# A four-layer gated cross-attention kernel: the order of single engine parts, down products by tokens, norms in pairs, and one product on GpSimd

## The chip, the cores and the metric

The kernel runs on one core of one Trainium2 chip. Its time is in microseconds (us) on the device, from the start of the program to its end, the median of some runs. The profile is that of one execution, and its span goes from the first to the last instruction of the program.

The engines are TensorE (PE in the rows, PEld for its weight loads), VectorE (DVE), ScalarE (ACT), GpSimd (POOL) and SyncE (SP, which only issues transfers).

## The reference, cut to what matters

Two batch elements ("halves", b = 0 and 1) of 512 tokens by 128 features go through four layers, each a cross-attention and a feed-forward part, both added to `x` with a gain of tanh:

```python
x = x + jnp.tanh(g_xattn[0]) * _L0_xattn_ref(_layernorm(x), ctx, ctx, mask, ...)   # stage 0: 16 heads of 8, 77 keys
x = x + jnp.tanh(g_ffn[0]) * _L0_ffn_ref(_layernorm(x), w1, b1, w2, b2)            # stage 1: relu, width 512
x = x + jnp.tanh(g_xattn[1]) * _L1_xattn_ref(_layernorm(x), ctx, ctx, ...)         # stage 2
x = x + jnp.tanh(g_ffn[1]) * _L1_ffn_ref(_layernorm(x), ...)     # stage 3: 16 experts of 64, top 2, a shared part of 352
x = x + jnp.tanh(g_xattn[2]) * _L2_xattn_ref(_layernorm(x), ctx, ctx, ...)         # stage 4
x = x + jnp.tanh(g_ffn[2]) * _L2_ffn_ref(_layernorm(x), ...)     # stage 5: 32 experts of 32, top 1, relu twice
x = x + jnp.tanh(g_xattn[3]) * _L3_xattn_ref(_layernorm(x), ctx, ...)  # stage 6: slot attention, 3 GRU steps
x = x + jnp.tanh(g_ffn[3]) * _L3_ffn_ref(_layernorm(x), rhs)     # stage 7: product of int8 values
```

Nothing in it crosses from one half to the other, so the halves may run in any order against each other. Within a half each stage needs the one before.

## The kernel before, in words

All of `x` stays in SBUF as four tiles of 128 tokens for each half. A stage begins with `norm` (VectorE: four `bn_stats`, four `bn_aggr`; GpSimd: variance plus epsilon to the power of minus a half, L698 and L699), `norm_end` (VectorE: four tiles of `xn`, L1315) and `turn` (TensorE: four transposes, L838; ScalarE: the copy `xn_t`, features on the partitions). An attention then goes `query`, `maxima` (four steps; VectorE takes the maxima of 16 blocks, L1443), `max_rows`, `scores` (three steps, each four eviction instructions of ScalarE with the exponential), `values` (three steps of sums and values together), `sum_rows`, `spread` (reciprocal sums spread with four full fp32 products, `rinv_d` against the identity), `project`. A feed-forward part has first products (`hidden0`; `shared` and `experts`; `hidden2`) and down products (`down0`, `down_shared` and `down1`, `down2`). The down products leave features on the partitions: a chunk is one fp32 product of 512 columns with the weights as the stationary side. ScalarE copies the sum to SBUF, TensorE transposes it back (`back`, L956), and VectorE adds it to `x` (L1346, L1542). A GRU step (`it` = 0 to 2) is `square`, `slots_turn` (L1052), `slot_products` (VectorE L1575), `slot_scores` (L1079, VectorE L1581), `hidden`, `slot_inverse`, four steps `gru` (VectorE L1609 and L1610), `gru_r` (VectorE L1616, L1617), `gru_z` (ScalarE, then VectorE L1622: `z` times the old slots) and `gru_end` (VectorE L1626, L1627). The last stage (L1324 to L1330, L1639) rounds to int8 values on VectorE.

Every engine runs a list of steps in fixed order (`ORDERS`). `schedule()` makes these lists when the program is built, from costs written beside each step. It walks three streams (half 0, half 1, preparation) and takes a step of a stream only in that stream's own order, with a few steps marked `on` or `side` that may overlap. `LATER` moves each step by a number of tenths. PSUM has eight banks, dealt by the same planner. Where it expects TensorE to be idle for long ahead of a step that takes a bank, it puts in fillers: bf16 products of 512 columns of constants (`psum<-halves` in the rows), whose result nobody reads. There are 178 of them: 33 ahead of the first `slots_turn`, 72 from there to the last `gru`, 73 in the last stage. All matrix products go through the helper on L754, and most ScalarE copies through L1124. Transfers are issued by SyncE in one list.

## Time and profile before

| | |
|---|---|
| median of 3 runs | 361.77 us (360.57 to 361.87) |
| the profiled execution | 361.95 us |
| its span | 360.2 us |
| TensorE busy | 328.1 us, 91% |
| VectorE busy | 225.3 us, 63% |
| ScalarE busy | 136.9 us, 38% |
| GpSimd busy | 47.8 us, 13% |

Busy time of TensorE counts the fillers too, and each product up to its modelled end, so two products in a pipeline overlap.

### The profile page before, as it was taken

How to read it: one execution, taken by the hardware profiler on the slowest of the kernel's cores; microseconds unless marked ns; L12 is line 12 of the kernel's file. 1: busy time of each engine (PE TensorE's matmuls, PEld its weight loads, DVE VectorE, ACT ScalarE, POOL GpSimd, SP SyncE). 2: the span in 40 equal slices, each digit the busy share in tenths (PEclk: the TensorE clock that was granted, in tenths of full speed). 3: DMA queues.
4: the chain of work that ended last, by engine and by line, in shares of the span. 5: the costliest groups of instructions: out<-in, count | busy, mean ns of one | idle time of the engine just before them, and what ended most of it. 6: DMA issues, size and time to landing. Idle time of an engine off the chain costs nothing.

```text
span 360.2 us, 5043 instructions
## 1 busy us (share of the span) xinstructions
PE 328.1 (91%) x1843; PEld 175.3 (49%) x1843; DVE 225.3 (63%) x635; ACT 136.9 (38%) x287; POOL 47.8 (13%) x73
## 2 busy tenths in 40 slices
PE   0789989998888899999999997899999999999994
PEld 0455453463424543554444434455445677677442
DVE  2596574366628551677766728345353797798995
ACT  1226326331451565225321361711232366646200
POOL 6113112031010100010200020101021311101110
PEclk9999999998989999999999999999999999999998
DMA  7940000000000000000000300000000000000001
GB/s 195 354 198 0 2 0 2 1 0 3 0 2 0 2 0 0 2 0 1 1 2 0 118 11 0 2 0 2 0 0 0 2 1 2 0 2 0 0 14 47
DMA packets 6669, 8.68 MB, mean 24 GB/s; under 512 B 2907, under 2 KB 5493, under 8 KB 6389
## 3 DMA queue, kind: packets, MB, share of 16 engines
q1 hardware_dynamic: 6645, 8.37, 7.0%
q8 instruction: 15, 0.25, 0.3%
q14 instruction: 9, 0.07, 0.1%
HBM read 7.84 MB, written 0.52 MB: 23 GB/s over the span
## 4 chain that ended last, share of the span: by engine, by line
PE 76%; DVE 15%; ACT 6%; issue 1%; DMA 1%; SPq 0%; DVEq 0%; ACTq 0%
PE psum L754 68%; DVE mx L1443 6%; ACT wide L1124 4%; PE psum L838 3%; DVE wide L1610 1%; PE psum L956 1%; PE psum L874 1%; DMA w_attn<-in_attn 1%; PE psum L1052 1%; PE psum L1079 1%; ACT xn_t L1124 1%; PE psum L791 0%; DVE rinv_d L1452 0%; DVE wide L1575 0%; DVE rinv L1449 0%
## 5 line engine op out<-in xcount | busy, mean ns | idle before, releaser
L754 PE MATMUL psum<-xn_t,w_ffn 128*128 128x512 f32 (+1 forms) x136 | 66.6, 608 | 0.8 <-ACT xn_t L1124 0.8
L754 PE MATMUL psum<-wide,w_ffn 128*128 128x512 f32 (+1 forms) x92 | 47.4, 603 | 0.5 <-DVE wide L1535 0.3
L754 PE MATMUL psum<-halves 128*128 128x512 bf16 x178 | 43.9, 379 | 0.2 <-DVE q_lo L1435 0.2
L1443 DVE TENSOR_REDUCE mx<-psum 128x4 f32<-128x308 f32 x96 | 38.7, 471 | 7.3 <-PE psum L754 7.1
L1124 ACT ACTIVATE wide<-psum 128x512 f32<-128x512 f32 x72 | 36.6, 624 | 11.0 <-PE psum L754 10.8
L1124 ACT ACTIVATE q<-psum 128x512 f32<-128x512 f32 (+1 forms) x40 | 23.5, 594 | 44.1 <-PE psum L754 43.8
L754 PEld LDWEIGHTS psum<-xn_t,w_ffn 128*128 128x128 f32 (+1 forms) x136 | 24.9, 190 | 28.8 <-issue 25.9
L698 POOL TENSOR_SCALAR nw<-mv 128x4 f32<-128x4 f32 x16 | 3.6, 227 | 218.7 <-DVE mv L1309 218.7
L754 PEld LDWEIGHTS psum<-halves 128*128 128x128 bf16 x178 | 17.3, 99 | 17.2 <-issue 1.7
L1315 DVE TENSOR_SCALAR xn<-x,mv,nw 128x128 f32<-128x128 f32 x64 | 17.8, 347 | 10.9 <-POOL nw L699 10.7
L754 PE MATMUL psum<-w_attn,q 128*128 128x128 f32 x192 | 23.7, 276 | 0.2 <-DVE q L1459 0.2
L754 PEld LDWEIGHTS psum<-wide,w_ffn 128*128 128x128 f32 (+1 forms) x92 | 16.3, 192 | 15.0 <-issue 8.5
L754 PEld LDWEIGHTS psum<-w_attn,q 128*128 128x128 f32 x192 | 22.5, 192 | 2.0 <-issue 1.1
L1124 ACT ACTIVATE xn_t<-psum 128x512 f32<-128x512 f32 x18 | 11.1, 615 | 30.5 <-PE psum L838 16.5
L1124 ACT ACTIVATE wide<-psum,cols 128x512 f32<-128x512 f32 x12 | 8.2, 687 | 31.2 <-PE psum L754 31.2
L754 PE MATMUL psum<-wide,heads_of 128*32 128x512 f32 x144 | 20.0, 626 | 0.0
L754 PE MATMUL psum<-wide,v_cols 128*32 128x512 f32 x144 | 19.6, 614 | 0.0
L1528 DVE TENSOR_TENSOR wide<-q,psum 128x512 f32<-128x512 f32 x16 | 11.0, 685 | 11.4 <-PE psum L754 9.8
L754 PE MATMUL psum<-wide 78*128 78x386 f32 x48 | 17.8, 496 | 0.2 <-DVE wide L1598 0.2
L699 POOL TENSOR_TENSOR nw<-nw,minus_half 128x4 f32<-128x4 f32 x16 | 16.6, 1036 | 1.3
L1306 DVE BATCH_NORM_STATS2 stats<-x 128x6 f32<-128x128 f32 x64 | 13.9, 280 | 3.9 <-DMA x<-in_x 3.5
L1435 DVE SCALAR_TENSOR_TENSOR q_lo<-psum,cols,q_hi 128x512 fp32r<-128x512 f32 x6 | 4.5, 751 | 18.5 <-ACT q_hi L1180 18.5
(208 smaller groups left out, 492.5 us busy)
## 6 DMA issues: line engine op xcount, KB each, us to landing
w_ffn<-in_ffn SPq DMA_DIRECT2D x1, 2088.5 KB, 12.6
w_ffn<-in_ffn SPq DMA_DIRECT2D x1, 1104.0 KB, 5.0
w_attn<-in_attn SPq DMA_DIRECT2D x1, 640.0 KB, 8.1
w_attn<-in_attn SPq DMA_DIRECT2D x2, 288.0 KB, 5.8
x<-in_x SPq DMA_DIRECT2D x2, 256.0 KB, 3.1
w_ffn<-in_ffn SPq DMA_DIRECT2D x1, 512.0 KB, 6.7
out<-x SPq DMA_DIRECT2D x2, 256.0 KB, 2.3
rows<-in_rows SPq DMA_DIRECT2D x1, 468.0 KB, 6.0
```

The lines of the kernel that those rows point to most:

```text
L699: G.tensor_tensor(nw[:, b, 2, :], nw[:, b, 0, :], minus_half[:, :], ALU.pow)\
L754: return nc.tensor.matmul(out_, lhs, rhs, start=start, stop=stop, **kw)
L838: last = nc.tensor.transpose(bk[:, t * P:(t + 1) * P], (y if stage == 7 else xn)[:, b, t, :], ident)
L874: last = nc.tensor.transpose(bk[:, t * P:(t + 1) * P], mx[:, b, t, :], ident)
L956: last = nc.tensor.transpose(bk[:, t * P:(t + 1) * P], tile[:, b, t * P:(t + 1) * P], ident)
L1052: last = nc.tensor.transpose(bk[:, t * P:(t + 1) * P], slots[:, b, t, :], ident)
L1124: A.activation(dst, banks.bank(*name)[0:rows_, 0:cols_], fn, **kw).then_inc(drained["act"], 1)
L1306: last = V.bn_stats(stats[:, b, t, :], x[:, b, t, :])
L1315: last = V.tensor_scalar(xn[:, b, t, :], x[:, b, t, :], mv[:, b, t, 0:1], nw[:, b, 2, t:t + 1], ALU.subtract, ALU.mult)
L1435: V.scalar_tensor_tensor(q_lo[:, b, :], banks.bank("q", layer, b), col(f"bq{layer}"), q_hi[:, b, :].bitcast(F32), ALU.add, ALU.subtract).t ...
L1443: last = V.tensor_reduce(mx[:, b, t, lane_heads(g)], banks.bank("max", layer, b, t, g)[:, 0:GK].rearrange("p (h k) -> p h k", k=CTX), AX.X ...
L1528: V.tensor_tensor(wide[:, b, c, :], act_s[slot][:, b, :], banks.bank("e_u", b, c), ALU.mult)\
```

## The change

1. **The planner** takes single engine parts: one step of one engine, with a list of the parts that it must follow. There are no streams any more; whichever part ranks first is next, whatever half it is of. The rank has the time at which a part can begin, `LATER` (new numbers, now for each part) and a fifth of the length of the chain that follows it. A change of TensorE's tiling (whole array, rows, columns) is charged 0.095 in the plan. `sums` and `values` are steps of their own, so are `gate` and `up` (the two first products of a piece), and the three products of `hidden`.
2. **Down products by tokens**: the hidden values are the stationary side and the weights the moving one, four products of 128 columns in place of one of 512, on top of a product of zeros that clears the bank. The sum has tokens on the partitions, and VectorE adds it to `x` from PSUM: the copy on ScalarE and the transposes of `back` go (in stage 5 the ReLU on ScalarE stays). `spread` becomes four transposes.
3. **Norms in pairs** of tiles: GpSimd and `norm_end` begin after two tiles, so GpSimd has twice the instructions.
4. **`z` times slots** (six instructions) goes from VectorE to GpSimd. In the last stage ScalarE scales and rounds, VectorE clamps.
5. **Fillers** may stand ahead of any TensorE part, in the bank that is free first. There are 101: 28 ahead of the first `slots_turn`, 9 from there to the last `gru`, 64 in the last stage. Eight more products stand at the start.
6. **Transfers** have another order, the identity and the query weights first, `x` of half 1 later; the weights of stage 5 are loaded after both `down0`, over the masks and the weights of layer 0.

The core of the diff:

```diff
+LEAD = {("pe", "turn"): 0.3}
+LEFT = 0.2
+SWITCH = 0.095
...
 def schedule():
...
+    waiting = list(steps.values())
+    while waiting:
         best = None
...
+        for st in waiting:
+            if all(steps[key].end is not None for key in st.after):
+                at = max([steps[key].end for key in st.after], default=0.0) - LEAD.get(st.key[:2], 0.0)
+                at = max(at, free[st.engine], LOADED.get(st.key, 0.0))
+                if st.engine == "pe" and tiling(st.phase, st.args)[0] != tiled:
+                    at = max(at, free["pe"] + SWITCH)
...
+                if at < float("inf"):
+                    rank = at + st.later - LEFT * st.left
...
+        if st.engine == "pe":
+            units = units_of(st.phase, st.half, st.args)
+            if at > FILL_FROM:
+                (bank, earlier), since = banks.first_free(drained)
+                idle = at - max(free["pe"], since) - FILLER
+                if idle >= FILLER:
+                    fillers[st.key] = bank, earlier, int(idle / FILLER)
...
             load_x(0)
+            sp.dma_start(cols[:, :], a["cols"]).then_inc(loaded["cols"], 16)
+            sp.dma_start(consts[:, 0:P], a["consts"][:, 0:P]).then_inc(loaded["ident"], 16)
+            sp.dma_start(packs["attn0"][:, 0:wq_n], a["attn0"][:, 0:wq_n]).then_inc(loaded["wq0"], 16)
...
             for b in range(B):
-                sp.wait_ge(*banks.full("y", 3, b))
+                sp.wait_ge(*banks.full("out", 1, b))
...
+            def norm(b, stage, h):
+                tiles = slice(2 * h, 2 * h + 2)
+                pool.wait_ge(var_ready[b], 2 * stage + h + 1)
+                link(G.tensor_scalar(nw[:, b, 0, tiles], mv[:, b, tiles, 1], LN_EPS, None, ALU.add))
+                G.tensor_tensor(nw[:, b, 2, tiles], nw[:, b, 0, tiles], minus_half[:, tiles], ALU.pow)\
...
+            def gru_z(b, it):
+                pool.wait_ge(z_ready[b], it + 1)
+                G.tensor_tensor(kept[:, b, :, :], tz[:, b, :, :], slots[:, b, :, :], ALU.mult).then_inc(kept_ready[b], 1)
...
-                    last = mm(bk[:, t * P:(t + 1) * P], rinv_d[:, b, t, :], ident)
+                    last = nc.tensor.transpose(bk[:, t * P:(t + 1) * P], rinv_d[:, b, t, :], ident)
...
                 pe.wait_ge(*banks.emptied(source, b, i))
-                done = mm(bk, weights[0:n, i * D:(i + 1) * D], wide[0:n, b, at_, :], start=i == 0, stop=last)
+                if i == 0:
+                    mm(bk, zeros16[:, :], halves[:, 0:S], stop=False)
+                by_tokens(bk, wide[0:n, b, at_, :], weights[0:n, i * D:(i + 1) * D], last)
+
+            def by_tokens(bk, source, weights, last):
+
+                for t in range(T):
+                    done = mm(bk[:, t * P:(t + 1) * P], source[:, t * P:(t + 1) * P], weights, start=False,
+                              stop=last and t == T - 1)
...
-            def back(b, stage):
-
-                pairs = [("s_out", ("s_y", b), s_y_t)] if stage == 3 else []
-                for name, source, tile in pairs + [("out", ("y", stage, b), y_t)]:
-                    bk = start_unit(name, *([stage] if name == "out" else []), b)
-                    pe.wait_ge(*banks.emptied(*source))
-                    for t in range(T):
-                        last = nc.tensor.transpose(bk[:, t * P:(t + 1) * P], tile[:, b, t * P:(t + 1) * P], ident)
-                    last.then_inc(filled, 1)
...
+            pe.wait_ge(idle_made, 1)
+            for _ in range(WARM_UP):
+                mm(psum[:, BANKS - 1, :], idle_t[:, 0:P], idle_t[:, :])
             for phase, b, args in ORDERS["pe"]:
+                if ("pe", phase, b, *args) in IDLE_FILLERS:
+                    keep_warm(*IDLE_FILLERS["pe", phase, b, *args])
...
+            def scaled(b):
+                act.wait_ge(centre_ready[b], 1)
+                for t in range(T):
+                    last = A.activation(xn[:, b, t, :], x[:, b, t, :], ACT.Identity, bias=nw[:, b, 0, t:t + 1],
+                                        scale=nw[:, b, 2, t:t + 1])
```

How the change moves instructions shows at two places. A row names the line, the operation, what is written, what is read (the moving side first) and the shape.

TensorE, stage 3 of half 1, before: the first products of a piece (`w_ffn1`, `experts`), the product that spreads the router's weights (`sel1`, `weigh`) and a down product (`wide,w_ffn1`, `down1`) take turns, and a step of `maxima` (`keys_hi,q_hi`) of half 0 stand between.

```order
L754 MATMUL psum<-wide,w_ffn1 128x512
L754 MATMUL psum<-keys_hi,q_hi 128x308 x4
L754 MATMUL psum<-xn_t,w_ffn1 128x512 x2
L754 MATMUL psum<-comb_t,sel1 128x512
L754 MATMUL psum<-wide,w_ffn1 128x512
L754 MATMUL psum<-xn_t,w_ffn1 128x512 x2
L754 MATMUL psum<-comb_t,sel1 128x512
```

TensorE, stage 3, now: the end of the first products of half 0, after those of half 1, then `weigh` and `down1` of both halves in turns.

```order
L854 MATMUL psum<-xn_t,w_ffn1 128x512 x8
L1104 MATMUL psum<-consts,comb 32x128 x4
L854 MATMUL psum<-xn_t,w_ffn1 128x512 x2
L854 MATMUL psum<-halves,zeros16 128x512
L854 MATMUL psum<-w_ffn1,wide 128x128 x4
...
L854 MATMUL psum<-comb_t,sel1 128x512 x7
L854 MATMUL psum<-halves,zeros16 128x512
L854 MATMUL psum<-w_ffn1,wide 128x128 x4
L854 MATMUL psum<-comb_t,sel1 128x512
L854 MATMUL psum<-w_ffn1,wide 128x128 x4
```

Both halves now do stage 3 side by side, ahead of any attention of stage 4, with no filler among these rows.

VectorE, GRU, before: `slot_scores` of one half (L1581), `gru_r` of the other (L1616, L1617), `z` times slots (L1622), `slot_inverse` (L1597, L1598), `hidden` (L1588), `gru_end` (L1626, L1627) and `gru`.

```order
L1581 TENSOR_REDUCE nmax<-psum 77x1
L1616 TENSOR_TENSOR wide<-wide 128x512
L1617 TENSOR_TENSOR wide<-wide 128x512
L1622 TENSOR_TENSOR q<-wide,xn 128x512
L1588 SCALAR_TENSOR_TENSOR wide<-psum,hidden_bias 128x4x128
L1597 RECIPROCAL nmax<-nmax 77x1
L1598 TENSOR_SCALAR wide<-vw,nmax 78x386
L1626 SCALAR_TENSOR_TENSOR xn_t<-wide,xn_t 128x512
L1627 TENSOR_TENSOR xn<-q,xn_t 128x512
```

VectorE, GRU, now:

```order
L1679 TENSOR_TENSOR wide<-psum,nw 128x308
L1685 TENSOR_REDUCE nmax<-psum 77x1
L1720 TENSOR_TENSOR wide<-wide 128x512
L1721 TENSOR_TENSOR wide<-wide 128x512
L1701 RECIPROCAL nmax<-nmax 77x1
L1702 TENSOR_SCALAR wide<-vw,nmax 78x386
L1692 SCALAR_TENSOR_TENSOR wide<-psum,hidden_bias 128x4x128
L1728 SCALAR_TENSOR_TENSOR xn_t<-wide,xn_t 128x512
L1729 TENSOR_TENSOR xn<-q,xn_t 128x512
```

The product of `z` and the slots is gone from VectorE; the rest keeps nearly the same turns between the halves.

## Rows read from the trace of the kernel before

**Rows 1.** The page: busy time, share and instructions of each engine.
```profile
PE 328.1 (91%) x1843; PEld 175.3 (49%) x1843; DVE 225.3 (63%) x635; ACT 136.9 (38%) x287; POOL 47.8 (13%) x73
```

**Rows 2.** The page: chain that ended last, share of the span.
```profile
PE 76%; DVE 15%; ACT 6%; issue 1%; DMA 1%; SPq 0%; DVEq 0%; ACTq 0%
```

**Rows 3.** Windows: length; PE, PEld, DVE, ACT, POOL busy; granted clock.
```profile
77.40:122.80 45.40, 39.41 (x251) 18.03 (x248) 27.42 (x83) 16.51 (x32) 7.59 (x9) 0.92 0.00 1
122.80:204.80 82.00, 81.58 (x316) 38.96 (x316) 49.86 (x136) 31.16 (x52) 3.81 (x5) 1.00 0.01 3
204.80:271.60 66.80, 61.69 (x374) 30.89 (x374) 33.06 (x99) 25.93 (x52) 8.02 (x12) 1.00 0.04 15
271.60:338.40 66.80, 65.78 (x380) 44.72 (x379) 52.50 (x127) 32.73 (x92) 9.00 (x15) 1.00 0.00 1
84.50:88.00 3.50, 3.50 (x9) 1.23 (x8) 2.29 (x5) 0.00 (x0) 0.00 (x0) 0.51 0.02 5
```

**Rows 4.** Timeline of the start: start, length, engine, line, what, count.
```profile
8.28 0.79 DVE L679 TENSOR_TENSOR keys_hi<-k_hi,lane_mask 128x616 fp32r<-128x616 f32 x1
8.44 1.71 POOL L679 TENSOR_TENSOR keys_lo<-k_lo,lane_mask 128x616 fp32r<-128x616 f32 x1 [2.18 <-DVE k_lo L1357]
8.99 1.33 DVE L1361 TENSOR_SCALAR minus_max<-lane_mask 128x308 fp32r<-128x308 f32 x1
10.25 1.10 DVE L1315 TENSOR_SCALAR xn<-x,mv,nw 128x128 f32<-128x128 f32 x4
17.04 6.26 DVE L1443 TENSOR_REDUCE mx<-psum 128x4 f32<-128x308 f32 x16 [0.90 <-PE psum L754]
```

**Rows 5.** Groups by line: names, shapes, count; busy us, mean ns.
```profile
L754 PE MATMUL psum<-halves 128*128 128x512 bf16 x178 | 43.9, 379 | 0.2 <-DVE q_lo L1435 0.2
L754 PE MATMUL psum<-consts,rinv_d 128*128 128x128 f32 x48 | 6.7, 283 | 2.8 <-DVE mx L1443 2.5 <-DVE rinv_d L1452 0.3
L754 PEld LDWEIGHTS psum<-w_attn,q 128*128 128x128 f32 x192 | 22.5, 192 | 2.0 <-issue 1.1 <-DVE q L1459 0.8
L699 POOL TENSOR_TENSOR nw<-nw,minus_half 128x4 f32<-128x4 f32 x16 | 16.6, 1036 | 1.3
L1622 DVE TENSOR_TENSOR q<-wide,xn 128x512 f32<-128x512 f32 x6 | 4.1, 683 | 0.0
```

**Rows 6.** Timeline: one fp32 product and its follower; `slots_turn`; one set of `hidden`.
```profile
264.51 1.02 PE L754 MATMUL psum<-xn_t,w_ffn 128*128 128x512 f32 x2
265.37 0.38 PE L754 MATMUL psum<-nothot_t,halves 128*128 128x512 bf16 x1
271.63 0.60 PE L1052 MATMUL psum<-consts,xn 128*128 128x128 f32 x4
288.00 2.84 PE L754 MATMUL psum<-w_attn,q 128*128 128x128 f32 x24
```

**Rows 7.** Timeline, attentions: end of the first; an eviction set; a query; later scores.
```profile
62.84 1.04 PE L754 MATMUL psum<-wide,v_cols 128*32 128x512 f32 x8
102.42 2.06 ACT L1124 ACTIVATE wide<-psum 128x512 f32<-128x512 f32 x4
105.26 1.13 PE L754 MATMUL psum<-xn_t,w_attn 128*128 128x512 f32 x2
106.42 0.69 ACT L1180 ACTIVATE q_hi<-psum,cols 128x512 fp32r<-128x512 f32 x1 [1.94 <-PE psum L754]
204.75 0.50 PE L754 MATMUL psum<-q_lo,keys_hi 32*128 32x512 f32 x4
```

**Rows 8.** Timeline: first and last `gru` end of five half-steps; VectorE beside GpSimd.
```profile
287.67 0.62 DVE L1610 SCALAR_TENSOR_TENSOR wide<-psum,route_s,wide 128x384 f32<-128x384 f32 x1
337.84 0.62 DVE L1610 SCALAR_TENSOR_TENSOR wide<-psum,route_s,wide 128x384 f32<-128x384 f32 x1
56.28 1.28 POOL L707 TENSOR_TENSOR x<-x,gbias 128x512 f32<-128x512 f32 x1 [1.23 <-DVE xn L1315]
56.31 1.27 DVE L1407 TENSOR_SCALAR p_small<-p_small 77x2 int32<-77x2 int32 x1
```

More of the change, by code:

```diff
@@ new lines, in all_steps, with chain, step, of @@
+def all_steps():
+    steps = {}
+    def chain(b):
+        def step(phase, *args, after=(), then=None, **takes):
+            previous = list(after)
+            for engine, us in takes.items():
+                key = engine, phase, b, *args
+                steps[key] = Step(key, us, previous + (then or {}).get(engine, []))
+                previous = [key]
+        return step
+    prepare_steps(chain(PREPARATION))
+    for b in range(B):
+        half_steps(b, chain(b))
+    return steps
+def of(b):
+    return lambda engine, phase, *args: (engine, phase, b, *args)
@@ L162, in attention @@
+        step("max_rows", layer, after=[at("dve", "maxima", layer, T - 1)], pe=0.45, act=0.5)
         for j in range(NJ):
-            step("scores", layer, j, on=True, pe=0.95 if layer else 1.95, act=1.95, after=[(PREPARATION, "masks")])
+            ready = [at("act", "max_rows", layer), at("dve", "query", layer), prepared("pool", "keys_in", layer)]
+            if not layer:
+                ready.append(prepared("act", "masks"))
+            step("scores", layer, j, after=ready + in_order("pe", "scores", layer, j), pe=0.95 if layer else 1.95, act=1.95)
@@ L172, in stream_steps @@
+        step("sum_rows", layer, after=[at("act", "sums", layer, NJ - 1)], pe=0.44, dve=0.92)
+        step("spread", layer, after=[at("dve", "sum_rows", layer)], then={"dve": [at("act", "values", layer, NJ - 1)]},
+             pe=0.44, dve=0.6)
+        step("project", stage, layer, after=[at("dve", "spread", layer)], then={"dve": [at("pool", "bias", stage)]},
+             pe=0.88, dve=0.65)
+        norm(stage + 1, [at("dve", "project", stage, layer)])
     norm(0)
     attention(0, 0)
-    step("bias", 1, side=True, pool=1.2, after=[(PREPARATION, "out_bias")])
@@ L233, in stream_steps @@
[L233 to L247 removed]
+    bias(1)
+    turn(1)
+    for m in range(C0):
+        step("hidden0", m, after=[at("act", "turn", 1)] + in_order("pe", "hidden0", m), pe=0.86,
+             **{"act" if m % 2 else "dve": 0.62})
+        down("down0", m, C0, [at("act" if m % 2 else "dve", "hidden0", m)])
@@ new lines, in half_steps @@
+    norm(4, [at("dve", "back_shared"), at("dve", "back", 3)])
+    attention(4, 2)
+    turn(5)
+    step("router", after=[at("act", "turn", 5)], pe=0.92, dve=1.74)
+    step("choice_turn", after=[at("dve", "router")], pe=0.43, act=0.5, dve=0.33)
+    for c in range(C2):
+        step("hidden2", c, after=[at("act", "turn", 5)] + in_order("pe", "hidden2", c), pe=0.86)
+        step("choose", c, after=[at("pe", "hidden2", c), at("dve", "choice_turn")] + in_order("pe", "choose", c), pe=0.22,
+             **{"act" if c % 2 else "dve": 0.62})
+        down("down2", c, C2 + 1, [at("act" if c % 2 else "dve", "choose", c)])
@@ new lines, in half_steps @@
+    step("slots_back", after=[at("dve", "gru_end", ITERS - 1)], dve=0.65)
+    norm(7, [at("dve", "slots_back")])
+    turn(7)
+    step("quantised", after=[at("dve", "turn", 7), prepared("dve", "slots_in", 4)], pe=0.25, dve=1.83)
+def schedule():
+    steps = all_steps()
+    for b, tenths in LATER.items():
+        for st, later in zip([st for st in steps.values() if st.half == b], tenths):
+            st.later = later / 10
+    followers = {key: [] for key in steps}
+    for st in steps.values():
+        for key in st.after:
+            followers[key].append(st)
+    for st in reversed(list(steps.values())):
+        st.left = st.us + LANDS[st.engine] + max([other.left for other in followers[st.key]], default=0.0)
```

633 lines of the change are left out of this document (305 added, 328 removed), and 49 rows, old and new, of the table LATER.

## The prediction

> **What bounds the kernel now.** I read four views, from wide to narrow. The page says who is busy: TensorE 91% of the span, VectorE 63%, nobody else half [rows 1]. The chain that ended last says who sets the end: TensorE with 76% of it, VectorE 15% [rows 2]. So the time is TensorE's list, from the first maxima to the last GRU step. But its busy time holds 178 fillers, 43.9 us [rows 5], in which it waited for somebody. The windows show the rest by stages [rows 3]. From 122.8 to 204.8 (stage 3, mostly) it is busy 81.6 of 82.0: here only fewer products or better cover elsewhere help. In the two attention stretches (77.4 to 122.8 and 204.8 to 271.6) it is bare idle for 6.0 and 5.1 us, and in the first of them the granted clock, 0.92 on average, was at 0.51, the lower level of 1.2 GHz, from 84.5 to 88.0 and for as long again. In the GRU stretch (271.6 to 338.4) it looks full with 65.8 of 66.8, yet 72 fillers stand there (some 16 us), and VectorE has 52.5: that stretch is a chain between the engines, with VectorE the fullest that does real work. The last 21.8 us are VectorE's chain of the last stage.
>
> **The change, part by part.** I follow half 0 and half 1 down the new order to four marks and compare each with before. Unit prices: an fp32 product of 512 columns takes 0.86 (264.51 to 265.37), four transposes 0.45 in a stream and 0.60 alone, a filler or bf16 product 0.22 to 0.25 [rows 5, 6].
>
> *Products.* A down step is now four fp32 products of 128 columns. The nearest rows are `hidden`: 24 records in 2.84 us, 0.95 a set of eight with its end, so 0.90 in a stream [rows 6]; against 0.86 that is +0.04, for 48 steps +1.9. The product of zeros comes eight times, +1.8. `back` gives up eight sets of four transposes at 0.45, -3.6. `spread` gave 48 records in 6.7 us, 1.1 a set [rows 5], and becomes 0.6: six times -0.5, -3.0. Net -2.9 us of TensorE's list. The bounds are -5 (down step at 0.86) and 0 (at 0.95). The marks below use these prices, so this is not added once more. ScalarE loses six copies, and with `back` a hop between two engines at the end of each feed-forward part; that is in the marks below.
>
> *Mark 1, first maxima, now 17.04* [rows 4]. VectorE does xn (10.25) after the keys, and then turn, query and masks pass before the maxima. In the new order xn and the mask parts come first (1.1 and about 1.1 us), then the key parts (about 2.7 with the 1.33 of minus_max), then q_lo (0.75). The first norm is ready at about 6.3, the mask and xn take VectorE to about 9.3, so the maxima start near 12.8, with turn and query hidden behind the keys: -4.2. Bounds: -2 when the mask lands late, -6 when the keys need not wait. The norms in pairs I take at nothing: the power on GpSimd is 1.04 us for four columns [rows 5], and if two columns cost as much, the second pair is ready as late as all four were.
>
> *To mark 2, scores of stage 4, half 0, now 204.8* [rows 7]. The first attention of both halves ends now at 63.9 [rows 7], 46.9 after the maxima began, and its steps stay the same: 12.8 + 46.9 = 59.7, and 2.6 for the last spread and project, 62.3. Stage 1 of both halves: eight first products (6.9), eight down steps (7.2), zeros and a turn (1.0), and 1.9 of waits for half 1's norm: 79.3. Attention of stage 2: both halves enter it together, which is the weak place of this order. Turn 0.6, copy 0.6, query 1.13, q_hi 0.69, q_lo 0.75 and 16 maxima 6.3 are a chain of 10.1 with hardly a product beside it [rows 4, 7]. After it the scores, sums and values of both halves take about 21 (six score sets at 2.06 of ScalarE, twelve products sets at 0.86 of TensorE, overlapping): 110.4. Stage 3, per half: 22 first products 18.9, 11 down steps 9.9, eight router products 1.8, gates 0.9, two turns 0.9, zeros 0.4, together 32.8; both 65.6, with 1.8 left of the attention and 2 of waits: 179.8. Then the chain of 10.1 again and 2 for the rows of maxima: scores at 192. That is -12.8 against 204.8.
>
> *Mark 3, first slots_turn, now 271.6* [rows 6]. The stretch is 66.8 now. Out go one back and two spreads (1.5), turn, query and a maxima step of half 1, which here come ahead of the mark (1.5), and one down step that moves behind (0.9); in come zeros and 13 down steps at +0.04 (0.9): -3.0. The 5.1 bare idle is mostly the maxima of half 1 with nothing beside them; the new order has scores and sums of half 0 there, and I leave 1.4: -3.7. Mark 3 at 252.1, -19.5.
>
> *Mark 4, last gru, now 338.4.* Here 72 fillers become 9, but they filled waits, so I give them no price of their own. Five half-steps take 50.2 us [rows 8], 10.0 each, more than TensorE's products need, so VectorE's turn sets the pace. Six products of 0.683 leave it [rows 5], and I take these 4.1 us as the gain; the idle in its 66.8 stays. Mark 4 at 252.1 + 62.7 = 314.8. Bounds: -8 if half of VectorE's idle goes too, +3 if `gru_end` now waits for GpSimd, whose nearest row is 1.27 to 1.28 [rows 8].
>
> *The end.* One z product was in the last chain too, but that is counted. ScalarE's scaling and rounding replace about 1 us of VectorE and add hops; 64 fillers stand in front of products that VectorE makes late. I take -0.7, bounds -3 and +2. Span 314.8 + 21.8 - 0.7 = 335.9. Outside the span lie 1.75 us (361.95 - 360.2), so **337.7**; the profiled execution was 0.2 above the median, so 337.
>
> **The rivals.**
>
> *Forecast, as above: 337 (326 to 345), chance 0.50.*
>
> *The order gives half of it back, 0.22.* The lists are fixed, so every part that is late stops all behind it on its engine, products of the other half included; costs in the plan are not measured ones. For it: in the kernel before bare idle stood beside fillers in the attention stretches, and with fewer fillers the clock may fall more often [rows 3] (each time costs at most half of 3.5 us). Against it: 122.8 to 204.8 shows that such a list can run without a gap. Half of the 19.5 gained at mark 3: 347 (345 to 357).
>
> *GpSimd and VectorE block each other, 0.11.* Beside a GpSimd product of 1.28 us a VectorE instruction on 77x2 elements took 1.27 (56.28 and 56.31), and minus_max took 1.33 beside keys_lo; but keys_hi, with two inputs in SBUF as `gru_r` has, took 0.79 beside the same GpSimd product, no longer than its size [rows 4, 8]. If z times slots stops VectorE each time, six times 1.28 is +7.7: 345 (341 to 348). The Trainium skill, SBUF — State Buffer, "Who interferes with whom", says that a VectorE instruction with two SBUF inputs contends with a GpSimd instruction that reads SBUF. By that rule the sum would be 345. The trace agrees for minus_max and the small one, and speaks against it for keys_hi.
>
> *More than forecast, 0.12.* The waits that I left in the new order (2.6, 1.9, 2, 1.4) go, and half of VectorE's idle in the GRU with them: 11 to 12 us, 325 (316 to 327).
>
> *Slower: weight loads come out in the open, 0.03.* Each down step loads eight weights in place of two. A load is 192 ns [rows 5]; if it did not hide behind the product before it, a step would be 1.54 in place of 0.90, 48 steps +31: 368. It decides from 24.5 / 48 = 0.51 us per step on. Against it: `hidden` has the same loads and runs at 0.12 a record.
>
> *The order brings nothing, 0.02:* the halves wait for each other as now, 360 to 363.
>
> **How the numbers follow.** Under 360 by more than 0.5% (1.8 us, about what a measurement of this kernel tells from no change) lie the first four cases: 0.95. Same 0.02, slower 0.03. The range for 8 in 10 reaches from inside the fourth case (324) to the middle of the second (353).
>
> **What would show it.** TensorE's rows: down steps of eight records at 0.11 to 0.12 each; transposes in place of rinv_d products. First maxima near 12.8; scores of stage 4 near 192; first slots_turn near 252, last gru near 315. TensorE full in stage 3 without fillers; bare idle of some 8 us in the attention of stage 2, perhaps with the lower clock behind it. In the GRU, VectorE's 0.69 us instruction gone and a GpSimd one of 1.3 in its place, with the half-step at 9.3. Wrong would be: records of 0.19 us in the down steps; `gru_r` of over 1 us beside GpSimd; waits in stage 3 for VectorE, which must keep up with both halves at once.

## The result, and the profile after

| | before | after |
|---|---|---|
| median | 361.8 us (4 runs, 360.6 to 362.1) | 347.2 us (4 runs, 345.1 to 347.5) |
| profiled execution | 361.95 us, span 360.2 | 347.13 us, span 345.3 |

The ratio is 0.959, with a 95% interval of 0.955 to 0.963: 4.1% less time. The prediction was 337 (324 to 353). The direction held and the time lies in the range, but 14.7 us were gained where 24.8 were forecast. The number is that of my second case (347), and the rest of this document asks where the 10 us went.

The page of the changed kernel, busy time and chain, answers to [rows 1] and [rows 2].

```profile
PE 313.7 (91%) x2014; PEld 191.7 (56%) x2014; DVE 221.6 (64%) x622; ACT 139.2 (40%) x291; POOL 68.1 (20%) x113
PE 63%; DVE 21%; ACT 8%; POOL 4%; issue 3%; DVEq 0%; POOLq 0%; ACTq 0%
```

TensorE's busy time fell by 14.4 us, nearly as much as the time did (14.7), and its share is the same 91%. But the chain moved: TensorE's part went from 76% to 63%, VectorE's from 15% to 21%, and GpSimd, which was not in it, has 4%. GpSimd's own busy time rose from 47.8 to 68.1.

The marks of the prediction, in the timeline of the changed kernel: start, length, engine, line, what, count.

```profile
13.43 6.26 DVE L1551 TENSOR_REDUCE mx<-psum 128x4 f32<-128x308 f32 x16 [1.04 <-PE psum L854]
...
76.67 1.10 PE L943 MATMUL psum<-consts,xn 128*128 128x128 f32 x4
...
116.37 0.70 PE L854 MATMUL psum<-xn_t,w_ffn 128*128 128x512 f32 x1
...
184.61 1.10 PE L854 MATMUL psum<-xn_t,w_attn 128*128 128x512 f32 x2
...
196.86 0.50 PE L854 MATMUL psum<-q_lo,keys_hi 32*128 32x512 f32 x4 [0.28 <-DVE mx L1551]
...
257.84 0.60 PE L1163 MATMUL psum<-consts,xn 128*128 128x128 f32 x4
...
322.89 0.62 DVE L1714 SCALAR_TENSOR_TENSOR wide<-psum,route_s,wide 128x384 f32<-128x384 f32 x1
```

| mark | before | predicted | after | missing in this stretch |
|---|---|---|---|---|
| first maxima | 17.0 | 12.8 | 13.4 | +0.6 |
| stage 1 done by both halves | | 79.3 | 76.7 | -3.2 |
| stage 3 entered | | 110.4 | 116.4 | +8.6 |
| stage 3 done by both | | 179.8 | 184.6 | -1.2 |
| scores of stage 4, half 0 | 204.8 | 192.0 | 196.9 | +0.1 |
| first `slots_turn` | 271.6 | 252.1 | 257.8 | +0.9 |
| last `gru` ends | 338.4 | 314.8 | 323.5 | +3.0 |
| end of span | 360.2 | 335.9 | 345.3 | +0.7 |

The last column is the length of the stretch that ends at the mark, measured minus predicted. Two stretches hold most of the miss: the attention of stage 2 with 8.6 us, of which 3.2 had been found before it, and the GRU with 3.0.

Windows of the changed kernel show what bounds them (length; PE, PEld, DVE, ACT, POOL busy; granted clock; DMA). The rows are the first and second part of the attention of stage 2, stage 3, stage 4 to `slots_turn`, the GRU stretch, and inside it a gap of TensorE and what came soon behind it.

```profile
76.67:97.20 20.53, 14.74 (x108) 7.25 (x106) 16.20 (x45) 7.30 (x13) 4.46 (x7) 0.94 0.16 56
97.20:116.37 19.17, 18.96 (x176) 7.40 (x172) 6.62 (x20) 10.55 (x20) 1.85 (x4) 0.97 0.00 1
116.37:184.60 68.23, 68.19 (x338) 44.74 (x335) 45.79 (x135) 25.42 (x45) 4.77 (x9) 1.00 0.00 1
196.86:257.80 60.94, 57.59 (x426) 35.04 (x427) 28.11 (x81) 24.23 (x50) 6.17 (x13) 1.00 0.00 1
257.80:323.50 65.70, 58.50 (x354) 44.52 (x354) 50.38 (x113) 34.16 (x93) 17.95 (x22) 0.95 0.00 1
286.20:288.06 1.86, 0.41 (x3) 0.04 (x1) 1.82 (x4) 0.84 (x3) 0.64 (x1) 1.00 0.00 0
290.20:296.00 5.80, 5.80 (x23) 4.73 (x22) 3.01 (x8) 3.41 (x11) 1.21 (x3) 0.50 0.01 3
```

Stage 3 is as predicted: TensorE busy 68.19 of 68.23 at full clock, no wait for VectorE. The attention of stage 2 has two parts. In the first, VectorE's norms and maxima are the fullest list (16.2 of 20.5 busy), and TensorE is bare idle (idle, with no filler either) for 5.8; I had expected some 8 in the whole attention. In the second TensorE has 18.96 of 19.17: it is mostly TensorE's own list that ends this attention, not the evictions (e11 below). In the GRU the shape is that of before (VectorE 50.4 of 65.7; [rows 3] had 52.5 of 66.8), with less cover on TensorE (7.2 bare idle, where it was 1.0) and a clock of 0.95 where it was 1.00: from 290.2 to 296.0 it stands at 0.50, the lower level of 1.2 GHz, soon after 1.86 us in which TensorE was busy for 0.41.

A half-step is one GRU step of one half; there are six, and I measure them from the end of one `gru` to the end of the next. VectorE in two of them, and GpSimd beside it:

```profile
275.18 0.68 DVE L1720 TENSOR_TENSOR wide<-wide 128x512 f32<-128x512 f32 x1
275.90 1.64 DVE L1721 TENSOR_TENSOR wide<-wide 128x512 f32<-128x512 f32 x1
...
275.01 1.98 POOL L823 TENSOR_TENSOR q<-wide,xn 128x512 f32<-128x512 f32 x1 [2.18 <-ACT wide L1382]
...
297.51 0.68 DVE L1720 TENSOR_TENSOR wide<-wide 128x512 f32<-128x512 f32 x1
298.22 0.69 DVE L1721 TENSOR_TENSOR wide<-wide 128x512 f32<-128x512 f32 x1
...
295.99 1.26 POOL L823 TENSOR_TENSOR q<-wide,xn 128x512 f32<-128x512 f32 x1 [3.48 <-ACT wide L1382]
```

The first three rows overlap: the first product of `gru_r` keeps its 0.68, the GpSimd product stretches from 1.26 to 1.98 (by about that 0.7), and the second product of `gru_r`, which ends 0.55 after GpSimd, takes 1.64 in place of 0.69. The sum of the three alone is 2.63, and from 275.01 to 277.54 they take 2.53, hardly less than one after the other. In the last three rows nothing overlaps and each has its own length. Of six half-steps three are of the first kind (275.0, 284.9, 306.3). The one between them (GpSimd at 296.0) is the half-step in which the clock was low: there `gru_r` came 1.5 us after the GpSimd product and missed it. In e3 below, at full clock, it is blocked too, and four of six are of the first kind. "`gru_r` of over 1 us beside GpSimd" was on my list of signs of being wrong. The Trainium skill, "SBUF — State Buffer", section "Who interferes with whom", has this as a rule: a VectorE instruction with two SBUF inputs contends with a GpSimd instruction that reads SBUF, and the contention is an exclusive lock. Here the trace agrees for the second product of `gru_r` (0.69 became 1.64) but not for the first, which began 0.17 after GpSimd and kept its 0.68 while GpSimd's record grew. I had given this rival 0.11, with keys_hi of [rows 4] against it; why that one was not held up stays open. The two rows that I counted for the rule, `minus_max` and the small one, read a single tensor in SBUF, so the rule as I cited it does not speak of them; they resemble `slot_inverse` in e2 below.

### The profile page after: what moved, and what is told of

Read it like the earlier page. It is cut to its first block, busy times and chain, and to the rows that moved or that the text cites. A ratio compares the mean times of both kernels' runs of the same rounds, so it can differ in the third digit from the quotient of the medians.

```text
span 345.3 us, 5466 instructions
## 1 busy us (share of the span) xinstructions
PE 313.7 (91%) x2014; PEld 191.7 (56%) x2014; DVE 221.6 (64%) x622; ACT 139.2 (40%) x291; POOL 68.1 (20%) x113
## 4 chain that ended last, share of the span: by engine, by line
PE 63%; DVE 21%; ACT 8%; POOL 4%; issue 3%; DVEq 0%; POOLq 0%; ACTq 0%
PE psum L854 56%; DVE mx L1551 7%; ACT wide L1238 4%; POOL nw L794 2%; PE psum L943 2%; ACT wide L1356 1%; DVE wide L1721 1%; DVE xn L1427 1%; PE psum L981 1%; ACT xn L1297 1%; DVE stats L1414 1%; DVE wide L1720 1%; DVE x L1454 1%; PE psum L1037 1%; PE psum L1029 1%
## 5 line engine op out<-in xcount | busy, mean ns | idle before, releaser
L854 PE MATMUL psum<-xn_t,w_ffn 128*128 128x512 f32 (+1 forms) x88 | 40.2, 595 | 0.0
L1238 ACT ACTIVATE q<-psum 128x512 f32<-128x512 f32 (+1 forms) x36 | 21.3, 594 | 31.3 <-PE psum L854 26.2
L854 PE MATMUL psum<-wide 78*128 78x386 f32 (+1 forms) x56 | 23.0, 544 | 6.0 <-DVE wide L1702 4.8
L854 PE MATMUL psum<-xn_t,early 128*128 128x512 f32 x52 | 26.9, 619 | 0.7 <-ACT xn_t L1238 0.7
L854 PEld LDWEIGHTS psum<-early,wide 128*128 128x128 f32 x192 | 24.3, 191 | 4.5 <-issue 3.8
L854 PE MATMUL psum<-halves 128*128 128x512 bf16 x101 | 25.1, 379 | 0.6 <-DVE wide L1577 0.4
L854 PE MATMUL psum<-early,wide 128*128 128x128 f32 x192 | 24.9, 276 | 0.0
L794 POOL TENSOR_TENSOR nw<-nw,minus_half 128x2 f32<-128x2 f32 x32 | 23.9, 746 | 2.7
L854 PEld LDWEIGHTS psum<-w_ffn,wide 128*128 128x128 f32 (+1 forms) x176 | 22.2, 192 | 3.1 <-issue 2.6
L1427 DVE TENSOR_SCALAR xn<-x,mv,nw 128x128 f32<-128x128 f32 x56 | 16.7, 342 | 10.3 <-POOL nw L794 10.2
L854 PE MATMUL psum<-w_ffn,wide 128*128 128x128 f32 (+1 forms) x176 | 22.4, 275 | 0.0
L1626 DVE TENSOR_TENSOR wide<-q,psum 128x512 f32<-128x512 f32 (+1 forms) x22 | 14.7, 684 | 11.0 <-ACT q L1238 10.3
L854 PE MATMUL psum<-wide,v_cols 128*32 128x512 f32 x144 | 19.5, 611 | 0.0
```

The costliest lines, as they stand in the source:

```text
L794: G.tensor_tensor(nw[:, b, 2, tiles], nw[:, b, 0, tiles], minus_half[:, tiles], ALU.pow)\
L854: return nc.tensor.matmul(out_, lhs, rhs, start=start, stop=stop, **kw)
L1238: A.activation(dst, banks.bank(*name)[0:rows_, 0:cols_], fn, **kw).then_inc(drained["act"], 1)
L1427: V.tensor_scalar(xn[:, b, t, :], x[:, b, t, :], mv[:, b, t, 0:1], nw[:, b, 2, t:t + 1], ALU.subtract, ALU.mult).then_inc(xn_ready[b], 1)
L1626: V.tensor_tensor(wide[0:r, b, at_, :], act_s[k % 2][0:r, b, :], banks.bank("up", b, k)[0:r, :], ALU.mult)\
```

## The experiments

All edits are of the changed kernel, except in e5. Each ratio is to the kernel before, run on the same chip in turns with it (360.9, 361.9 and 360.9 us in the three sets: e1 to e4, e5 to e8, e9 to e12). The changed kernel has 0.959 (0.955 to 0.963), to 361.8 us. Since the kernel before differs by up to 1.0 us between the sets, differences of medians across them are good to about 1 us, and the ratios are the better measure.

**e1, z times slots back on VectorE.**

```diff
             def gru_z(b, it):
-                pool.wait_ge(z_ready[b], it + 1)
-                G.tensor_tensor(kept[:, b, :, :], tz[:, b, :, :], slots[:, b, :, :], ALU.mult).then_inc(kept_ready[b], 1)
+                pass
...
                 V.tensor_tensor(tr[:, b, :, :], tr[:, b, :, :], gates[:, b, :, 2 * D:3 * D], ALU.add)\
                  .then_inc(n_in_ready[b], 1)
+                dve.wait_ge(z_ready[b], it + 1)
+                V.tensor_tensor(kept[:, b, :, :], tz[:, b, :, :], slots[:, b, :, :], ALU.mult).then_inc(kept_ready[b], 1)
```

> The changed kernel with the product of z and the old slots back on VectorE, right behind gru_r. Theory A (they block each other): in the changed kernel the second instruction of gru_r takes 1.64 us in place of 0.69 in three of six half-steps, each time beside the GpSimd product. Here all six are 0.69, VectorE pays 0.69 for the product in the five half-steps of the GRU stretch and gets 3 x 0.95 back: the GRU stretch is 0.6 us longer at most, the time 347.8 (346 to 349). Theory B (the block costs nothing, since the half-step waits for other engines): the stretch stays or gets longer by what VectorE now does more, up to 5 x 0.69 = 3.4 us: 350.6.

Measured 349.0 (346.4 to 350.2), ratio 0.967 (0.962 to 0.971). All six second products of `gru_r` are 0.69. The middle half-steps, from the end of one `gru` to the next, take 9.5 us (284.3, 293.8, 303.3), where the changed kernel has 9.9 with a block at full clock (273.0 to 282.9). So VectorE is faster with its own product than with the block, and Theory B is out. The time was longer all the same, and in the trace it is the clock that took it:

```profile
77.00:97.00 20.00, 14.37 (x93) 6.93 (x96) 16.10 (x45) 6.15 (x11) 4.38 (x6) 0.91 0.17 58
280.00:310.00 30.00, 25.49 (x157) 19.12 (x158) 26.09 (x58) 18.78 (x56) 3.60 (x6) 1.00 0.00 1
310.00:324.00 14.00, 10.37 (x48) 6.92 (x48) 9.05 (x22) 5.09 (x13) 1.20 (x2) 0.81 0.01 2
```

The profiled execution of e1 lost 1.7 us in the attention of stage 2, where its code is the same, and its last half-step (313.8 to 326.5) took 12.7 us, where the changed kernel has 8.1. The mean clock from 310 to 324 was 0.81. Over the six runs the time goes with the mean clock of the run: 346.4 us at 0.978, 350.2 at 0.962. I had not put a price on that.

**e2, the GpSimd product behind `gru_r`.**

```diff
                 pool.wait_ge(z_ready[b], it + 1)
+                pool.wait_ge(n_in_ready[b], it + 1)
...
                 dve.wait_ge(n_ready[b], it + 1)
-                dve.wait_ge(kept_ready[b], it + 1)
                 dve.wait_ge(z_ready[b], it + 1)
                 link(V.scalar_tensor_tensor(nn[:, b, :, :], tz[:, b, :, :], 1.0, nn[:, b, :, :], ALU.subtract, ALU.mult))
+                dve.wait_ge(kept_ready[b], it + 1)
```

> The changed kernel with the GpSimd product of z and slots waiting for the end of gru_r, and gru_end waiting for it only ahead of its second instruction. Theory A: gru_r is 0.69 twice in all six half-steps, three half-steps lose 0.95 us each: 347.2 - 2.9 = 344.3. Theory B: VectorE's next instructions (slot_inverse, gru_end) take the block in place of gru_r, or the chain goes past VectorE: 347.2, within 1 us. Theory C (the clock sets the GRU stretch): what a quicker half-step gives is taken back by where the clock falls, 346 to 349.

Measured 351.3 (348.8 to 352.5), ratio 0.973 (0.969 to 0.977): 4 us slower than the changed kernel by the medians and 5 by the ratios, not 3 faster. My Theory A was half of the truth. The block is real, but moving the product only chooses whom it hits. e4 below has the same edit with full clock in the GRU, and there VectorE and GpSimd read:

```profile
287.88 0.69 DVE L1726 TENSOR_TENSOR wide<-wide 128x512 f32<-128x512 f32 x1
288.49 0.15 DVE L1706 RECIPROCAL nmax<-nmax 77x1 f32<-77x1 f32 x1
288.68 1.52 DVE L1707 TENSOR_SCALAR wide<-vw,nmax 78x386 f32<-78x386 f32 x1
...
288.71 1.27 POOL L828 TENSOR_TENSOR q<-wide,xn 128x512 f32<-128x512 f32 x1 [3.91 <-DVE wide L1726]
```

Now it is `slot_inverse` that takes 1.52 us in place of 0.42, and TensorE's `gru` products wait for just that. Theory B's first half (the next instructions take the block) is shown. Theory C came on top: in the profiled execution of e2 the clock had a mean of 0.54 from 290 to 300, and the GRU stretch is 67.8 us (65.7 in the changed kernel, and 64.3 in e4, whose clock stayed up). The last stage is 23.1 us (21.8), at a mean clock of 0.91. In e4 it is 23.0; there the first of its norms is done 0.3 us later after the last `gru` than in the changed kernel, which is the edit's own price, and the other 0.9 is lost behind it, where the mean clock is 0.68 (336 to 340). Which part of the 4 us is the clock's alone these runs don't separate.

**e3, more fillers in the GRU.** The planner puts in a given number of fillers ahead of named steps, in the bank that is free first:

```diff
+FORCED = {('pe', 'gru', 1, 0, 0): 5, ('pe', 'gru', 0, 1, 0): 5, ('pe', 'gru', 1, 1, 0): 5, ('pe', 'gru', 0, 2, 0): 4, ('pe', 'gru', 1, 2, 0): 2, ('pe', 'slot_products', 0, 1): 2, ('pe', 'slot_products', 1, 0): 2, ('pe', 'slot_products', 1, 1): 2, ('pe', 'slot_products', 0, 2): 2, ('pe', 'slot_products', 1, 2): 2}
...
+                if st.key in FORCED:
+                    bank, earlier = banks.first_free(drained)[0]
+                    fillers[st.key] = bank, earlier, fillers.get(st.key, (0, 0, 0))[2] + FORCED[st.key]
```

> The changed kernel with 31 more fillers in the GRU stretch, in the idle time ahead of the gru products (5, 5, 5, 4, 2) and ahead of slot_products (2 each), up to what stood idle there. Theory C (too few fillers): the granted clock stays up in the whole stretch (now 0.69 from 290 to 300), the half-step of 11.5 us becomes 9.8: 345.5. Theory A: the three blocks stay at 1.64 us. Rival: the fillers delay the products behind them, 348 to 349.

Measured 345.8 (345.1 to 346.9), ratio 0.958 (0.955 to 0.962). Its window of the stretch, and of the piece that was bad:

```profile
257.80:321.80 64.00, 61.63 (x378) 44.81 (x385) 51.23 (x113) 34.02 (x93) 18.59 (x22) 1.00 0.00 1
290.00:300.00 10.00, 9.57 (x58) 6.86 (x59) 8.71 (x18) 6.17 (x19) 3.11 (x3) 1.00 0.01 2
```

Theory C holds in the trace: clock 1.00 to the end of the stretch, which takes 64.0 in place of 65.7, and every middle half-step 9.8 to 9.9 with the block in it: the second product of `gru_r` is 1.64 or 1.65 in four half-steps, not in three as I expected. In the medians that is 1.4 us less, but 0.9 of it is the kernel before being faster in this set, and the ratios (0.958 and 0.959) are the same.

**e4, both edits** (with 17 fillers, seven of them ahead of `gru`).

> Both edits together: the GpSimd product behind gru_r, and 16 more fillers ahead of the gru products and slot_products. Theories A and C together: -2.9 and -1.7 from 347.2 = 342.6, GRU stretch 61 us in place of 65.7. If only one of them holds, 344.3 or 345.5.

Measured 347.1 (346.0 to 349.2), ratio 0.962 (0.958 to 0.966). The clock stayed up in the GRU, but with the block at `slot_inverse` each middle half-step is 10.0 us. In the profiled executions e4 is 3.5 us behind e3: 0.3 in the GRU stretch (0.1 to 0.2 a half-step), 1.2 in the last stage (23.0 against 21.9, most of it with the lower clock, as under e2), and 2.0 before the GRU, where its code is the same and the clock fell in the attention of stage 2. So of the two theories C holds by itself, and A's cure does not.

**e5, the kernel before with `spread` by transposes.**

```diff
-                    last = mm(bk[:, t * P:(t + 1) * P], rinv_d[:, b, t, :], ident)
+                    last = nc.tensor.transpose(bk[:, t * P:(t + 1) * P], rinv_d[:, b, t, :], ident)
```

> The kernel before with one edit: spread as four transposes in place of four fp32 products against the identity. By my sum each of the six sets is 0.5 us shorter, all on the path: 3.0 us less than the kernel before. Rival: only the sets that nothing waits beside count; the spreads stand at the ends of attentions where TensorE is otherwise idle or filled for others, so that 1 us or less is left of it.

Measured 362.7 (360.7 to 363.5, 12 runs), ratio to the kernel before 1.003 (1.0005 to 1.005): nothing gained, if anything a microsecond lost. The rival holds. In the profiled executions the scores of stage 4 come at 203.0 against 204.8, and the first `slots_turn` at 271.3 against 271.6: what had been won was given back in the next attention. There (205 to 232 us) the clock was 0.87 where it was 1.00. The mean clocks of the 12 runs are 0.980 to 0.990, those of the kernel before in the same set 0.985 to 0.997. Why the clock falls there is not shown; that the shorter product leaves more idle time is only a guess. I had sold TensorE's saving at its full price.

**e6, norms not in pairs.** GpSimd takes the four columns in the second step of a norm, `norm_end` the four tiles.

```diff
-                pool.wait_ge(var_ready[b], 2 * stage + h + 1)
-                link(G.tensor_scalar(nw[:, b, 0, tiles], mv[:, b, tiles, 1], LN_EPS, None, ALU.add))
+                if h == 0:
+                    return
+                pool.wait_ge(var_ready[b], 2 * stage + 2)
+                link(G.tensor_scalar(nw[:, b, 0, :], mv[:, b, :, 1], LN_EPS, None, ALU.add))
...
-                for t in range(2 * h, 2 * h + 2):
+                for t in range(T):
```

> The changed kernel with one norm of four columns on GpSimd and four tiles of xn together, as before; the first of each pair of steps does nothing on GpSimd and in norm_end. My forecast took the pairs at nothing: 347, within 1. Rival: in the changed kernel the power takes 0.72 on two columns and 1.01 on four, so the last xn ends about 0.6 us later than in pairs; where the norm is on the path (some eight of sixteen) that makes up to 5 us: 352. As a side effect a longer wait of TensorE may bring the lower clock.

Measured 349.9 (349.2 to 351.0), ratio 0.969 (0.966 to 0.973): the pairs are worth 2.7 us by the medians and 3.6 by the ratios, where I had taken them at nothing. The norm of stage 1, half 0, in e6, from the first statistics on:

```profile
60.67 0.49 DVE L1416 BATCH_NORM_STATS2 stats<-x 128x6 f32<-128x128 f32 x2
...
62.18 0.23 POOL L795 TENSOR_SCALAR nw<-mv 128x4 f32<-128x4 f32 x1 [11.69 <-DVE mv L1419]
62.56 1.04 POOL L796 TENSOR_TENSOR nw<-nw,minus_half 128x4 f32<-128x4 f32 x1
63.63 1.11 DVE L1431 TENSOR_SCALAR xn<-x,mv,nw 128x128 f32<-128x128 f32 x4 [1.54 <-POOL nw L796]
```

and in the changed kernel:

```profile
60.53 0.49 DVE L1414 BATCH_NORM_STATS2 stats<-x 128x6 f32<-128x128 f32 x2
...
61.69 0.72 POOL L794 TENSOR_TENSOR nw<-nw,minus_half 128x2 f32<-128x2 f32 x1
62.44 0.60 DVE L1427 TENSOR_SCALAR xn<-x,mv,nw 128x128 f32<-128x128 f32 x2 [0.49 <-POOL nw L794]
...
62.69 0.72 POOL L794 TENSOR_TENSOR nw<-nw,minus_half 128x2 f32<-128x2 f32 x1
63.44 0.60 DVE L1427 TENSOR_SCALAR xn<-x,mv,nw 128x128 f32<-128x128 f32 x2 [0.40 <-POOL nw L794]
```

The power takes 0.72 on two columns and 1.04 on four. From the first statistics to the last `xn` it is 3.51 in pairs and 4.07 whole, and in pairs the first two tiles are there a microsecond sooner. By the marks e6 is 1.4 behind at the first turn of stage 2 (78.0 against 76.7) and 3.7 at the scores of stage 4 (200.6 against 196.9), part of it again through the clock in the attention (0.86 from 85 to 97, against 0.91). In the last stage it is the other way: from the last `gru` to the end e6 takes 21.3 us, the changed kernel 21.8.

**e7, no charge for a change of tiling** (`SWITCH = 0.0`).

> The changed kernel with the planner's charge for a change of tiling at zero and the same table of numbers. The order of TensorE changes in one place only (a step of maxima of stage 2 moves up by one), the three other engines' orders not at all, with 8 more fillers. 347, within 1 us. If it is more than 2 us off, small moves around the attention of stage 2 matter more than all I counted.

Measured 349.6 (345.9 to 350.6, 3 runs), ratio 0.966 (0.959 to 0.972). Two of the runs are 2.4 and 3.4 us above the median of the changed kernel, one is 1.3 below it; I had expected 347 within 1. With a single step of 352 moved, the orders of the three other engines alike and the intervals overlapping, I don't read this as a price of the charge. The profiled execution differs where the step is and where the clock is: 0.86 from 85 to 97, stage 3 entered 2.3 us later, and 0.66 from 290 to 300.

**e8, more fillers in the attention of stage 2**: as e3, ahead of six steps of `maxima`, `query` and `scores` and one `turn`.

> The changed kernel with 19 more fillers in the idle time of the attention of stage 2 (77 to 97 us), up to what stood idle there. If the lower clock from about 94 to 98 comes of this idle time, it goes, and stage 3 is entered 1.7 us sooner, and the runs scatter less: 345.5. Rival: the fillers stand ahead of products that VectorE and ScalarE wait for and delay them, or the clock falls all the same: 347 to 349.

Measured 347.3 (346.7 to 347.7), ratio 0.961 (0.958 to 0.965). The windows of e8:

```profile
77.00:97.00 20.00, 16.85 (x119) 7.99 (x122) 15.47 (x43) 6.75 (x13) 4.38 (x6) 1.00 0.16 58
97.00:117.00 20.00, 19.79 (x186) 7.88 (x179) 6.62 (x20) 11.79 (x24) 1.84 (x4) 1.00 0.00 1
```

The clock stays up in this attention, and the runs lie within 1.0 us of each other instead of 2.4. But half 1's turn of stage 3 comes at 113.70 against 113.93, and since e8 also entered the attention 0.4 sooner (76.24 against 76.67), full clock bought nothing in the profiled execution. Where the clock fell ahead of the first scores the price differs: the turn of stage 3 came 1.7 to 2.3 later in e1, e4 and e7, 0.7 later in e9, and not at all later in e3. So the 8.6 us are not the clock's. It may make the scatter, but that is not shown: e3, with the lower clock there, lies within 1.8 us.

**e9, z times slots on VectorE at the head of `gru_end`, and 20 fillers in the GRU; e10, the same with the fillers of e8.**

> The changed kernel with z times slots on VectorE again, at the head of gru_end (behind slot_inverse and hidden, not ahead of them as in e1), and with 20 more fillers in the GRU stretch. e1 showed half-steps of 9.5 us while the clock was up, e3 9.85 with the GpSimd product and its three blocks. If VectorE's own instructions set the half-step, it is 9.5 here too, at full clock to the end: GRU stretch 63.5, the time 344.5. Rival: slot_inverse comes 0.69 sooner than in e1 and TensorE's part of the half-step was on the path: 9.0, 342. If the clock falls all the same: 347.

> e9 and the 19 fillers in the attention of stage 2 as well. e8 had the full clock in that stretch and entered stage 3 at 113.70 against 113.93, but scattered by 1 us where others scatter by 2 to 5. If the lower clock in the attention is chance from run to run, this one loses nothing in its best runs and wins in its middle ones: 343.5, scatter of 1 us. Rival: no difference from e9.

Measured 347.2 (346.3 to 349.8), ratio 0.964 (0.960 to 0.968), and 346.4 (346.0 to 346.8), ratio 0.961 (0.957 to 0.965). Full clock in the whole GRU stretch, no block, and middle half-steps of 9.7 us: 0.15 less than e3 with its blocks. From the first to the last `gru` end both take 48.8 us, and e3 48.9. The product costs VectorE about as much at its own place (0.68, six times) as the block does (0.95, in four of six in e3). From the last `gru` to the end e9 and e10 take 22.9 and 22.7 us, the changed kernel 21.8. Only about 0.15 us of that is there when the first norm of the last stage is done; the rest comes behind it, where the clock fell (a mean of 0.57 from 332 to 336 in e10). Neither beats the changed kernel or e3. e10 is the steadiest of those with several runs (0.8 us between its six).

**e11, fewer products in the attention of stage 2.**

> The changed kernel without two of three steps of values in the attention of stage 2 of both halves (left out: 32 products, four sets of eight with 0.88 us each, so the output of that attention is of the last chunk of keys alone). Theory D (TensorE's list sets the end of that attention from 97 us on, where it is busy 19.8 of 20.0): stage 3 is entered 2.6 us sooner or more, the time is 344. Theory E (ScalarE's six evictions of 2.06 and the waits for banks set it): under 1 us sooner, 346.5 to 347.

Measured 346.2 (343.9 to 347.6), ratio 0.960 (0.955 to 0.965). The total says little, since in this execution the clock fell in both stretches. The marks tell the theories apart. From half 1's first scores to its turn of stage 3:

```profile
91.45 0.80 PE L854 MATMUL psum<-q_lo,keys_hi 32*128 32x512 f32 x4
113.77 0.44 PE L943 MATMUL psum<-consts,xn 128*128 128x128 f32 x2
```

22.3 us. In e1 and e4, which also had the lower clock there, it is 24.5 (91.15 to 115.67 in e1), in the changed kernel 24.3 (89.64 to 113.93), in e8 24.1, and 24.0 at the least in any other run. So 3.5 us of TensorE's products less make this stretch 1.7 to 2.2 shorter. That is nearer to Theory D (2.6) than to E (under 1), though it is neither: TensorE's list is the larger part of what ends this attention, and waits between the engines take the remainder.

**e12, the planner without its table** (`LATER = {}`).

> The changed kernel with all numbers of LATER at zero: the same parts, costs, ranks and charge for tiling, but no hand in the order. If the single parts and the rank carry the gain, 350 to 365. If the order comes from the table, the halves run into each other's waits and the time is well over the kernel before: 400, with more than 300 fillers.

Measured 419.7 (419.3 and 420.0), ratio 1.164 (1.157 to 1.172), with 342 fillers. Without its table the changed kernel, with everything else that is new in it, is 16% slower than the one before; the 14.7 us are those of the new parts together with an order that the table gives. How they divide among the order, the down products by tokens and the transfers was not tried: no run changes one of these alone.

## Why the prediction was right in direction and short in size

**Marks 1 and stage 3: right.** First maxima 13.4 against 12.8; stage 3 at 68.2 us, within 1.2 us of its sum, without a filler or a wait for VectorE. A set of eight down records takes 0.89, by the 32 records of half 0 in stage 1:

```profile
73.10 3.73 PE L854 MATMUL psum<-early,wide 128*128 128x128 f32 x32
```

The rival of exposed weight loads (0.03) is refuted: 0.11 a record.

**Stage 1: too pessimistic by 3.2 us.** The first attention and the feed-forward part fit closer than I had it. I had priced the norm pairs at nothing, and e6 shows 1.4 us up to the first turn of stage 2, 2.7 in all. That term was wrong, in my disfavour. The rest of the 3.2 stays open (the same code reached this mark at 76.0 to 76.9 in the other runs). So two misses of opposite sign partly cancel: that the total is 10 us off and not 13 is luck.

**The attention of stage 2: the step that failed.** I wrote that "both halves enter it together, which is the weak place of this order", and priced it at 10.1 for the chain and "about 21" for the rest. Measured are 13.0 (76.67 to 89.64) and 26.7 (to 116.37). The chain lacked the rows of maxima and their copy (1.3), which I had put in at stage 4 and not here, and the add, norm and `xn` of half 0, which stand in VectorE's list ahead of half 1's maxima: they begin at 81.68, where the q_hi products were done at 80.9. In the rest I added up ScalarE's six sets (12.4) and the twelve sums and values (10.3) and let them overlap, and left out TensorE's other work: six steps of scores at 1.2, the transposes of rows and sums, `spread` and `project`, some 12 us more. With them TensorE alone is busy for 24.0 of the 26.7 us. From 97.2 on it is busy 18.96 of 19.17, and e11 shows that its list is the larger part of what ends this attention. Ahead of 97.2 there is a wait that I hadn't seen coming:

```profile
90.84 2.06 ACT L1238 ACTIVATE wide<-psum 128x512 f32<-128x512 f32 x4 [1.50 <-PE psum L854]
93.00 0.41 PE L854 MATMUL psum<-keys_hi,q_hi 32*128 32x308 f32 x4 [1.78 <-ACT wide L1238]
93.23 0.50 PE L854 MATMUL psum<-q_lo,keys_hi 32*128 32x512 f32 x4
```

A step of scores holds four banks, a step of maxima holds four, and there are eight. The maxima of half 0 at 93.00 wait 1.78 us for banks that half 1's evictions empty at 92.9, and half 1's next scores stand behind them. Two halves in one attention share the banks, not only the engines. What an order without that wait would give was not tried: with one number of the table moved, the planner changes the rest of the order too.

**To mark 3: right** (61.0 against 60.1).

**The GRU: the gain of 4.1 became 1.1.** The product left VectorE, as predicted, but in three of six half-steps (four at full clock) its place was taken by a block of 0.95 us. e1, e2 and e4 show that this is the product on GpSimd and follows it to whichever instruction stands beside it; e9 and e10 show that on VectorE at full clock it costs about the same, so the move is worth nothing measurable in the half-step. And "72 fillers become 9, but they filled waits, so I give them no price" was wrong: the clock fell to the lower level soon after a gap of TensorE, the half-step there took 11.1 in place of 9.9, and e3 gets 1.7 us back in the profiled stretch by filling. So 1.7 of the 3.0 us missing here are the clock's. At full clock the stretch is 64.0 (e3), 2.8 shorter than before and not 4.1, and the middle half-step that I had put at 9.3 is 9.8 to 9.9. Even these 2.8 are not the product's: e9 and e10, with it on VectorE, take 63.9. No run singles out what in the new order gives them.

**The end: no gain** (21.8 against 21.1). In the first half of the last stage GpSimd's power took 1.09 and 1.20 us beside VectorE's `gru_end` and add, against 0.72 alone, and the last GpSimd product of `z` and the slots (1.30, at 325.52) stands ahead of them in the chain that ended last. With whole norms (e6) the stage is 0.5 shorter. What each of these costs by itself was not measured.

```profile
327.09 1.09 POOL L794 TENSOR_TENSOR nw<-nw,minus_half 128x2 f32<-128x2 f32 x1
328.50 1.20 POOL L794 TENSOR_TENSOR nw<-nw,minus_half 128x2 f32<-128x2 f32 x1
```

**The prices.** "Net -2.9 us of TensorE's list" rested for 3.0 us on `spread`. As a price of the products it is right (0.60 to 0.66 a set at full clock in e5), but e5 shows that nothing of it reaches the end when it is made alone.

**Of the rivals**, the number is that of the second (347), but its mechanism, half of the gain at mark 3 lost, isn't what happened: 5.7 of 19.5 were lost there, by my own sum; the match is luck. The block between GpSimd and VectorE came true in half of its places, at 0.95 each instead of 1.28, and on both engines.

## What to carry to other kernels

Before two halves are put into the same phase, add up for each engine everything that both do there, the small transposes too, and count the banks; overlap is what is left after the fullest list. A product that moves from VectorE to GpSimd with inputs in SBUF is not free for VectorE: look which instructions will stand beside it, since the block goes along with it. And fillers have a price when they are taken away: where a chain between engines leaves TensorE idle in every round, look at the granted clock behind the gaps before pricing them at nothing.

## What the runs showed of the hardware

- Two VectorE products and one GpSimd product on SBUF, 0.68, 0.69 and 1.26 alone (2.63), took 2.53 together in the changed kernel. A VectorE instruction that reads one tensor and one column of SBUF was held up beside the GpSimd product too (0.42 became 1.52, e2 and e4).
- The granted clock stood at 0.50 (1.2 GHz) from 290.2 to 296.0 in the changed kernel, after TensorE had been busy for only 0.41 us from 286.20 to 288.06. A half-step earlier (276.20 to 278.20, busy 0.56 of 2.00) such a gap was passed without a fall. From run to run of one program the mean clock differs: 0.962 to 0.978 in e1, with times of 350.2 to 346.4 us. In e10, with fillers in both stretches, it differs by about as much (0.982 to 0.996), but the times lie between 346.8 and 346.0.
